# Router logits of three expert nets, made in their norm stage straight from the turned tokens, with the bias in one addition

## The reference, cut to what matters

```python
# first net: layernorm, router, softmax, the best expert, scaled by its probability
# second net: layernorm, router, the best expert (argmax of the logits)
logits = x @ router_w + router_b            # (4096, 128) @ (128, 8) + (8,)
# third net: the experts choose the tokens
xn = x_flat * jax.lax.rsqrt(jnp.mean(x_flat * x_flat, axis=-1, keepdims=True) + EPS) * norm_weight
logits = xn @ router_w.T + router_b
probs = jax.nn.softmax(logits, axis=-1)
gates, idx = jax.lax.top_k(probs.T, cap)    # cap = 512
```

## Time and profile before

| | |
|---|---|
| median of 3 runs | 4927.64 us (4926.19 to 4941.84) |
| the profiled execution | 4930.94 us, with a span of 4929.2 us |
| TensorE busy, matmuls | 3808.5 us of the span (77%) |
| TensorE busy, weight loads | 2743.6 us (56%) |
| VectorE busy | 2777.7 us (56%) |
| ScalarE busy | 2343.5 us (48%) |
| GpSimd busy | 1509.0 us (31%) |
| mean granted TensorE clock | 0.873 of full speed |

### The profile page before, as it was taken

How to read it: one execution, slowest core, us unless ns; L and a number is a source line. 1 busy time by engine, 2 the same in 40 slices (tenths; PEclk the granted TensorE clock), 3 DMA queues, 4 the chain that set the end, 5 groups by cost and what they waited for, 6 DMA issues and landing times. The chain is left out here.

```text
span 4929.2 us, 93708 instructions
## 1 busy us (share of the span) xinstructions
PE 3808.5 (77%) x28449; PEld 2743.6 (56%) x28449; DVE 2777.7 (56%) x6429; ACT 2343.5 (48%) x6756; POOL 1509.0 (31%) x1134
## 2 busy tenths in 40 slices
PE   0776866588999957669979999778874366959986
PEld 0554852265777756457757777533334244727764
DVE  4776555455777669222227777689993412435553
ACT  1333431387777644334446666455542014537763
POOL 0211010001656555000005555378880050105420
PEclk9777967699999979869989999899985587979988
DMA  5000000022222100000001111044432024900000
GB/s 178 7 6 4 6 0 4 20 81 66 68 66 67 56 6 0 5 26 0 0 8 30 30 29 30 23 155 138 138 120 72 13 46 122 209 11 0 0 0 21
DMA packets 165117, 229.69 MB, mean 47 GB/s; under 512 B 58786, under 2 KB 130381, under 8 KB 162134
## 3 DMA queue, kind: packets, MB, share of 16 engines
q1 hardware_dynamic: 159342, 223.67, 15.7%
q0 software_dynamic: 5632, 4.33, 0.7%
HBM read 201.64 MB, written 9.45 MB: 43 GB/s over the span
## 5 line engine op out<-in xcount | busy, mean ns | idle before, releaser
L2810 PE MATMUL l2a_pY<-l2a_hc,ident 128*128 128x512 f32 x512 | 273.3, 672 | 91.1 <-POOL l2a_hc L2727 56.5
L2258 ACT ACTIVATE l2x_att_prob<-l2x_att_pS,l2x_att_nmx 128x257 f32<-128x257 f32 x512 | 236.3, 474 | 209.0 <-DVE l2x_att_nmx L2294 209.0
L2114 POOL TENSOR_TENSOR l2x_att_prob<-l2x_att_prob,l2x_att_rs 128x1028 f32<-128x1028 f32 x128 | 243.4, 1901 | 273.3 <-DVE l2x_att_rs L2299 273.3
L2114 POOL TENSOR_TENSOR l1x_att_prob<-l1x_att_prob,l1x_att_rs 128x1028 f32<-128x1028 f32 x128 | 243.4, 1902 | 206.3 <-DVE l1x_att_rs L2299 206.3
L2258 ACT ACTIVATE l1x_att_prob<-l1x_att_pS,l1x_att_nmx 128x257 f32<-128x257 f32 x512 | 236.3, 474 | 147.1 <-DVE l1x_att_nmx L2294 147.0
L2697 POOL TENSOR_TENSOR l2a_dbu<-l2a_dx,l2a_BC 128x1024 f32<-128x1024 f32 x128 | 298.7, 2354 | 20.5 <-PE l2a_pY L2810 10.6
L2827 ACT ACTIVATE l2a_pA<-l2a_dl,l2a_A 128x512 f32<-128x512 f32 x256 | 174.6, 689 | 187.7 <-DVE l2a_pH L2933 112.7
L2810 PEld LDWEIGHTS l2a_pY<-l2a_hc,ident 128*128 128x128 f32 x512 | 103.7, 211 | 252.4 <-issue 119.1
L2310 DVE COPY l1x_att_probT<-l1x_att_pT 86x512 f32<-86x512 f32 x256 | 175.5, 686 | 116.2 <-PE l1x_att_pT L2200 107.9
L2933 DVE TENSOR_TENSOR_SCAN l2a_pH<-l2a_pA,l2a_dbu 128x512 f32<-128x512 f32 x192 | 224.8, 1217 | 23.3 <-POOL l2a_dbu L2697 11.9
L1610 POOL TENSOR_TENSOR l3a_att_kb<-l3a_KA,l3a_att_own_head 128x2048 f32<-128x2048 f32 x32 | 154.8, 4840 | 266.4 <-PE l3a_att_pS L1644 155.7
(11 more groups left out here) (688 smaller groups left out, 10348.2 us busy)
## 6 DMA issues: line engine op xcount, KB each, us to landing
l2a_BC<-l2a_rows SPq DMA_DIRECT2D x128, 512.0 KB, 3.8
l3x_att_ctn<-ctx_n SPq DMA_DIRECT2D x32, 576.0 KB, 12.4
l0x_sum_ctx<-ctx_t SPq DMA_DIRECT2D x16, 1028.0 KB, 4.9
l1x_k_xin<-ctx_t SPq DMA_DIRECT2D x32, 514.0 KB, 3.5
l1x_att_ctx<-ctx_t SPq DMA_DIRECT2D x128, 128.5 KB, 2.1
l1x_att_kT<-l1x_KA SPq DMA_DIRECT2D x128, 128.5 KB, 2.2
l2x_att_ctx<-ctx_t SPq DMA_DIRECT2D x128, 128.5 KB, 2.1
l3x_att_ctx<-ctx_t SPq DMA_DIRECT2D x32, 514.0 KB, 10.5
```

The source lines that it names most:

```text
L2114: pool.tensor_tensor(p, p, bc(rs[:, b, :], 2, KEYS), ALU.mult).then_inc(scaled, 1)
L2258: last = act.activation(prob[:, b, j, 0:KEYS], pS[:, j, 0:KEYS], ACT.Exp, bias=nmx[:, b, j:j + 1], accum_out=sums[:, b, j:j + 1])
L2810: last = pe.matmul(pY[c][:, :], env.ident[:, :], hc[:, u % 3, c, :], start=False, stop=n == NS - 1)
```

## The change

The router's matmuls move out of `route` into `normalise`. A new function, `router_inputs`, opens rw, rb and a PSUM bank pl for the logits of all 32 tiles, and loads rw and rb in a block of its own ahead of the norm; rb is now spread over all 128 partitions. TensorE waits for both ahead of its first transpose. From group 4 of the transposes on it puts behind each group the logits of the group four back, read straight from XNT; the last four groups of logits follow at the end. The matmuls with the bias are gone. `route` starts with one addition of pl and rb into LG. For the kind "choice" the probabilities go straight to W, without the reduction and the copy. The turned weights are copied by ScalarE for even groups and by VectorE for odd ones. A stage around the norm and the router holds rw, rb and pl.

```diff
@@ normalise, TensorE
+                def logits(g):
+                    pe.wait_ge(copied, g + 1)
+                    for n in range(g * TG, (g + 1) * TG):
+                        pe.matmul(router.pl[:, n * EXPERTS:(n + 1) * EXPERTS], dst_t[:, n * P:(n + 1) * P],
+                                  router.rw[:, :])
+
+                if router is not None:
+                    pe.wait_ge(router.ready, 32)
                 for g in range(GROUPS):
...
                     last.then_inc(turned, 1)
+                    if router is not None and g >= 4:
+                        logits(g - 4)
+                if router is not None:
+                    for g in range(GROUPS - 4, GROUPS):
+                        logits(g)
+
+def router_inputs(nc, st, names):
+    r = Names(rw=st.sb("rw", [P, EXPERTS]), rb=st.sb("rb", [P, EXPERTS]), pl=st.ps("pl", [P, 512]),
+              ready=st.sem("ready"))
     rw_d, rb_d = names
+    with nc.Block() as block:
+        @block.sync
+        def _(sp):
+            sp.dma_start(r.rw[:, :], rw_d).then_inc(r.ready, 16)
+            sp.dma_start(r.rb[:, :], bc(rb_d.rearrange("o e -> (o e)"), 0, P)).then_inc(r.ready, 16)
+    return r
@@ route, ScalarE
-                with act.Fori(0, GROUPS // 2) as i:
-                    for s in range(2):
-                        act.wait_ge(logits[s], before(i))
-                        act.activation(xs[:, s, :], env.XNT[:, bass.ds((2 * i + s) * 512, 512)], ACT.Copy
-                                       ).then_inc(xs_ready[s], 1)
...
-                for g in range(GROUPS):
+                for g in range(0, GROUPS if WT is not None else 0, 2):
@@ route, TensorE
-                with pe.Fori(0, GROUPS // 2) as i:
-                    for s in range(2):
-                        pe.wait_ge(xs_ready[s], made(i))
-                        pe.wait_ge(kept[s], before(i))
-                        for t in range(TG):
-                            o = pl[s][:, t * EXPERTS:(t + 1) * EXPERTS]
-                            pe.matmul(o, xs[:, s, t * P:(t + 1) * P], rw[:, :], start=True, stop=False)
-                            last = pe.matmul(o, env.ones[0:1, 0:P], rb[:, :], start=False, stop=True)
-                        last.then_inc(logits[s], 1)
...
-                        pe.wait_ge(w_kept, g - 1)
+                        pe.wait_ge(w_kept if g % 2 == 0 else dve_kept, g // 2)
@@ route, VectorE
-                with dve.Fori(0, GROUPS // 2) as i:
-                    for s in range(2):
-                        dve.wait_ge(logits[s], made(i))
-                        dve.tensor_copy(LG[:, bass.ds((2 * i + s) * TG, TG), :],
...
+                dve.wait_ge(router.ready, 32)
+                done(dve.tensor_tensor(LG[:, :, :], router.pl[:, 0:TILES * EXPERTS].rearrange(
+                    "p (n e) -> p n e", e=EXPERTS), bc(router.rb[:, :], 1, TILES), ALU.add))
                 done(dve.tensor_reduce(m[:, :], LG[:, :, :], AX.X, ALU.max))
...
+                    if kind == "choice":
+                        done(dve.tensor_tensor(W[:, :, :], l0[:, :, :], bc(rs[:, :], 2, EXPERTS), ALU.mult))
...
+                for g in range(1, GROUPS if WT is not None else 0, 2):
+                    dve.wait_ge(w_turned, g + 1)
+                    dve.tensor_copy(WT[:, g * 512:(g + 1) * 512], pw[g % 2][0:EXPERTS, :]).then_inc(dve_kept, 1)
@@ l0_ffn; l1_ffn and l2_ffn alike
-    normalise(nc, env, "l0f_ln", env.X, dst_t=env.XNT)
...
-        route(nc, env, "l0f_route", (a.L0_ffn_router_w, a.L0_ffn_router_b), W, WT, "max")
+        with stage(nc, "l0f_logits") as inner:
+            router = router_inputs(nc, inner, (a.L0_ffn_router_w, a.L0_ffn_router_b))
+            normalise(nc, env, "l0f_ln", env.X, dst_t=env.XNT, router=router)
+            route(nc, env, "l0f_route", router, W, WT, "max")
```

More of the change, by code:

```diff
@@ L97, in bc, with normalise @@
     return a.to_broadcast(shape)
-def normalise(nc, env, title, src, dst_t=None, dst=None, gain=None, shift=None, again=None, onto=None, table=None, first=None):
+def normalise(nc, env, title, src, dst_t=None, dst=None, gain=None, shift=None, again=None, onto=None, table=None, first=None,
+              router=None):
     CHUNKS = 4
@@ L293, in route @@
         rs = st.sb("rs", [P, TILES])
[L294 to L297, removed]
+        pw = [st.ps(f"pw{s}", [P, 512]) for s in range(2)]
+        dve_step, exp_done, w_ready, w_turned, w_kept, dve_kept = (st.sem(n) for n in (
+            "dve_step", "exp_done", "w_ready", "w_turned", "w_kept", "dve_kept"))
         with nc.Block() as block:
@@ L336, in _ @@
                 pe.wait_ge(w_ready, 1)
-                for g in range(GROUPS):
+                for g in range(GROUPS if WT is not None else 0):
                     if g >= 2:
-                        pe.wait_ge(w_kept, g - 1)
+                        pe.wait_ge(w_kept if g % 2 == 0 else dve_kept, g // 2)
                     for t in range(TG):
-                        last = pe.transpose(pl[g % 2][0:EXPERTS, t * P:(t + 1) * P], W[:, g * TG + t, :],
+                        last = pe.transpose(pw[g % 2][0:EXPERTS, t * P:(t + 1) * P], W[:, g * TG + t, :],
@@ L373, in _ @@
                     src = LG
-                if kind == "choice":
-                    done(dve.tensor_copy(W[:, :, :], pr[:, :, :]))
-                else:
+                if kind != "choice":
                     first_of_max(dve, done, env, src, m, l0, rs, W)
@@ L739, in l1_ffn @@
 def l1_ffn(nc, env, a):
-    normalise(nc, env, "l1f_ln", env.X, dst_t=env.XNT)
     with stage(nc, "l1f") as st:
@@ L743, in l1_ffn @@
         WT = st.sb("WT", [EXPERTS, T])
-        route(nc, env, "l1f_route", (a.L1_ffn_Wr, a.L1_ffn_br), W, WT, "one")
+        with stage(nc, "l1f_logits") as inner:
+            router = router_inputs(nc, inner, (a.L1_ffn_Wr, a.L1_ffn_br))
+            normalise(nc, env, "l1f_ln", env.X, dst_t=env.XNT, router=router)
+            route(nc, env, "l1f_route", router, W, WT, "one")
         w = Names(w1=a.L1_ffn_W1, b1=a.L1_ffn_b1, w2=a.L1_ffn_W2, b2=a.L1_ffn_b2)
@@ L1014, in _ @@
                              a.L2_ffn_fc2_b.rearrange("e d -> (e d)").unsqueeze(0)).then_inc(fetched, 16)
-        normalise(nc, env, "l2f_rms", env.X, dst_t=env.XNT, gain=gain[:, 0:1], again="rms", table=by_tile(table)[:, :, 0:D],
-                  first=(landed, 32))
-        route(nc, env, "l2f_route", (a.L2_ffn_router_w, a.L2_ffn_router_b), W, WT, "choice")
+        with stage(nc, "l2f_logits") as inner:
+            router = router_inputs(nc, inner, (a.L2_ffn_router_w, a.L2_ffn_router_b))
+            normalise(nc, env, "l2f_rms", env.X, dst_t=env.XNT, gain=gain[:, 0:1], again="rms",
+                      table=by_tile(table)[:, :, 0:D], first=(landed, 32), router=router)
+            route(nc, env, "l2f_route", router, W, WT, "choice")
         choose_tokens(nc, env, "l2f_choose", WT, PT)
```

23 lines of the change are left out of this document (6 added, 17 removed).

## The result

The changed kernel takes 4844.35 us (median of 5 runs, 4838.33 to 4850.08) where the kernel before takes 4926.65 on the same chip: a ratio of 0.9829, interval 0.9814 to 0.9845. Timed in two more series beside other kernels, the changed kernel gave 4840.3 (ratio 0.9833, 0.9812 to 0.9854) and 4848.63 (0.9848, 0.9831 to 0.9864), so the gain is between 72 and 82 us by the series.

The account below looks back on a forecast made before the run. Stages add up; ScalarE ends the norm stages and TensorE's logits bound the router stages. Gains of 19.2 + 19.9 + 19.0 = 58.1 us take 4930.9 to 4872.8, written 4869 for a median; range 4850 to 4884.

Parts of the forecast that it names:

- Removed: Router stages: the 32 bias matmuls go, 32 x 0.524 = 16.8 us in each of three nets, all on the path.
- Moved: Norm stages: the other 32 matmuls at 0.524 us join the transposes; TensorE ends the stage, which grows by 14.6 us.
- rival 2: Third net waits longer, 4877, or mixing transposes and logits costs extra, 4873 to 4877; both 4881 to 4885; chance 0.16.
- (a): Start of the router stage: one 128x256 addition of the bias from PSUM, 0.46 us with its step.
- (b): Ahead of the norm: a block that loads the router's inputs, 1.3 us, bounds 0.5 and 2.8.
- (c): One more block that clears semaphores, 0.45 us, nearly given back by fewer to clear in the router stage; 0.1 taken.
- (d): Copies of turned weights shared by ScalarE and VectorE: a loss of 0.3 us, bounds -1 and +1.
- (e): Router stage: the 1.28 us exp table load just hidden beside 1.35 us of other work; otherwise up to 1.3 in two nets.
- (f): Third net's router: a reduction and a copy go, a gain of 0.8 us.
- The wait in the third net: Third norm: router inputs land behind six transfers, TensorE starts at 3731.3, not 3724.55; on time would be 4.1 us better.
- Rival 1, the clock: Norm stages: TensorE's clock rises to 2.4 GHz, 9.1 us a net if for all logits, 4842 or 4855; chance 0.12.
- Rivals 2 to 4: Longer wait or dearer mix (0.16); stalled tiles, slower than before, 4946 (0.02); under 14.8 us gain, 4913 or above (0.02).

Follow-up runs that it names:

- run 2: Kernel before with its bias matmuls left out and the bias not added, logits still in the router's stage: 4858.81 us, ratio 0.9868.
- run 3: Kernel before, second matmul changed per net: alternating into own columns, grouped in fours, token product twice; passes 0.262, 0.224, 0.213 us apart, no whole time given.
- run 9: Changed kernel with router inputs at the head of the norm's or the six transfers' block and ScalarE alone copying turned weights: 4846.92 us against 4848.63.
- run 4: Changed kernel with the third net's router inputs issued ahead of the six large transfers: 4838.13 us, ratio 0.9845 against the kernel before.
- run 5: Changed kernel with TensorE held in all three norms until VectorE has applied three chunks: 4855.15 us, against 4840.3 for the changed kernel beside it.
- run 10: Five executions of the changed kernel varying the third net's input order and TensorE's start, two of them repeats: 4851.0, 4850.24, 4845.12, 4854.63, 4860.04 us.
- run 1: Changed kernel with the bias matmul put back behind each token matmul, in the norm stage: 4907.46 us, ratio 0.9967 against the kernel before.
- run 7: Changed kernel with all logits behind the last transpose instead of between the transposes: 4845.84 us in one run.

## Why the prediction was wrong, by its own steps

**Removed**: right in kind, too small. The forecast had 3 x 16.8 us for the bias matmuls and run 2 measured 60.7. By itself this doesn't move the sum, because the old stage's 33.56 us go whole in either case; the price of what stays behind does, and that is the next step.

**Moved**: the step that failed. "33.56 / 64 = 0.524 us a matmul" was measured on a stream that alternated weights of 128 rows and of one row, and was carried over to one that does not. It is a mis-sized term: the moved matmuls take 0.427 (two passes of 0.2134), and run 3 shows that the difference belongs to the alternation. From the end of group 4 to the end of TensorE's work the forecast had 19.6 us and the profile has 15.7 (680.91 to 696.60): 3.1 are the 64 passes and 0.6 the three groups of transposes between logits, each 0.745 beyond the 1.71 of eight passes and not 0.94 (the forecast's 2.82 / 12 counts the length of the last transpose too; their starts are 0.213 apart). It is worth 4 us in each net, 12 of the 19 us by which the three stages exceed the forecast (77.4 less 58.1). The clue stood in the forecast itself: rival 2 noticed that "a pass is 0.37 long and steps by 0.26" and asked what new changes would cost, and not what the old ones already had.

**The order of the stage**: right. Group 4 ends 13.06 us after the norm's start, as forecast to the hundredth; TensorE ends the stage, and the addition follows 1.61 later (1.56 forecast).

**Added.** (a) The addition takes 0.42 and its step 0.45 (0.46). (b) 1.20 and 1.22 us (1.3). (c) Nothing that can be seen. (d) 0.36 us lost in the first net (7.54 us from the first turn to the last copy's end, 7.18 before; 0.3 forecast); run 9 shows the same 0.35 at an equal clock. (e) The table load ends at 699.45 and the exponential starts at 699.57: hidden by 0.12, as forecast "just". (f) 2.85 us from the reduction to the first turn in place of 3.6: 0.8.

**The wait in the third net**: right in kind, 1.0 us better in size (18.3 for 19.3 from the first issue). By ring order as the Trainium skill has it (DMA: Bandwidth & Descriptors, section "Queues, rings and completion order") the small load had to come late; the trace agrees, with 12.5 us against 2.6 in run 4. At an equal clock the wait costs 2.6 us, worked out and not run: last logits start at 28.7 in run 4, and a start at 11.5 with the 19.8 us that run 5 shows from TensorE's start to its last pass (12.3 to 32.1) makes 31.3. The forecast had 4.1.

**Rival 1, the clock**: given 0.12 and dismissed by the rows of the norm and router at 0.50. It happened, in the third net of all three profiled executions of the changed kernel and in the second of one: 6.2 us in the profile, of the 11.3 by which that net beat the forecast; the others are 4.0 of passes and transposes and 1.0 of the landing. The rows that stood against it were of 8-column passes; the rise came during twelve or twenty unbroken transposes of 128 columns or within 0.7 us behind them, and in the profile after the clock fell again 2.6 us into the 40 unbroken passes at the end. The Trainium skill (TensorE: Matmul & The Clock Gate, Part 1) has activity release the clock, and the moment depend on where the first matmul falls against a window that runs free of the kernel. The traces agree with the second part: the rises and the missing ones of the first two nets part by where the row of possible changes stood (run 10). That 33.56 us of nearly unbroken 8-column matmuls stayed at 0.50 the page doesn't explain.

**Rivals 2 to 4** did not occur. A change between transposes and logits of 128 rows both costs nothing that can be seen: the period of 2.455 us (680.70 to 683.16) holds eight passes and four transposes, and twelve at the 0.2134 of unmixed passes would be 2.56.

**The sum.** 58.1 + 12 (passes and transposes) + 6.2 (clock) + 1.0 (landing) = 77.3, against 77.4 in the two profiles. The medians differ by 82.3, 81.8 and 72.4 in the three series. What lies between is not taken apart; a rise in the second net is worth 3 us, and two executions differed by 13.6 us before the first changed instruction, so the spread alone could make it.

Not shown is why the change costs 0.10 us; run 3 shows only that it goes with the number of changes between one row and 128, of the weights and of the moving operand together.

## What to carry to other kernels

A price taken as busy time over a count belongs to the mixture it was measured in: before it is carried to a new mixture, compare the distance of starts with the duration of one, and look for what in the old mixture could make the two differ. A bias of one row added by its own matmul behind every small matmul costs more than its passes; one addition of 128x256 for 0.42 us replaced 32 of them. And where TensorE is half idle in one stage and the bound of the next, moving is worth less than removing: here 12 to 16 us (run 1), beside 60.7 for leaving the bias matmuls out (run 2).

## What the runs showed of the hardware that was not expected

- Changing between matmuls of 128 rows and of one row costs about 0.10 us a change at 1.2 GHz (0.262 a pass in alternation, 0.224 in fours, 0.213 without), and shows in no instruction's duration.
- Eight passes of 128x8 are busy for 1.71 us at a granted clock of 0.50 and for 0.96 at 1.00, at the same place of the stream.
- The clock fell from 1.00 to 0.50 in the midst of unbroken 8-column passes (the profile after, 3682.6 us), and 13 us of them ran unbroken at 0.50 (run 7).
- The same stream at the same moment of a stage ran once at 0.50 and once risen (run 10), a difference of 6 us. All changes of the clock in a trace lie on one evenly spaced row of moments, and the two executions differ by 0.49 us in where it stands; twenty norms with one stream part the same way.
- A load of 4 KB behind 6 MB in one queue lands after 12.5 us, ahead of them after 2.6, and taking the wait away need not shorten the time.
